# Gated edge pass: the weighting of the gathered rows and the absolute value of the angle move from VectorE to ScalarE

## The reference

```python
# layer 1, per edge (row = source, col = destination): a gate from both ends, then a gated sum
edge_weights = sigmoid(relu(concat([h[row], h[col]]) @ We1 + be1) @ We2 + be2)
aggr = segment_sum(edge_weights[:, None] * h[row], col, num_segments=n)
# layer 3, per edge: the time encoding, from the node's last update and the edge's time
rel_t = last_update[src] - t
rel_t_enc = cos(rel_t[:, None] * Wt[0][None, :] + bt)          # 64 columns
edge_attr = concat([rel_t_enc, msg])                           # 64 + 64 columns
```

## Time and profile before

| | us |
|---|---|
| median of three runs | 13884.4 (13879.9 to 13896.82) |
| the profiled execution | 13875.03 |
| its span | 13873.3 |
| DVE busy | 10723.6 (77%) |
| PE busy | 8685.8 (63%) |
| POOL busy | 6951.8 (50%) |
| ACT busy | 2809.5 (20%) |
| the gated pass, about 6616 to 8025 | 1409 |

### The profile page before, as it was taken

How to read it: one execution, slowest core, us unless ns; L and a number is a source line. 1 busy time by engine, 2 the same in 40 slices (tenths; PEclk the granted TensorE clock), 3 DMA queues, 4 the chain that set the end, 5 groups by cost and what they waited for, 6 DMA issues and landing times. The chain is left out here.

```text
span 13873.3 us, 209115 instructions
## 1 busy us (share of the span) xinstructions
PE 8685.8 (63%) x52858; PEld 7028.6 (51%) x52859; DVE 10723.6 (77%) x16335; ACT 2809.5 (20%) x4518; POOL 6951.8 (50%) x7719
## 2 busy tenths in 40 slices
PE   4663577767778678773566636773666665666664
PEld 3552255553566446553555524552555554555554
DVE  7666479964899559985888867998677877677777
ACT  0110222223222232220444412221000000000000
POOL 3774057730777227760777706773344443344442
PEclk8555788878788788886888856665788888788887
DMA  4335754437444464451555612222233333333333
GB/s 179 113 112 131 266 165 105 104 53 295 112 105 104 113 260 106 105 93 28 141 147 145 141 23 51 54 54 23 86 96 92 93 95 69 95 93 93 95 93 65
DMA packets 720170, 1523.50 MB, mean 110 GB/s; under 512 B 364796, under 2 KB 416585, under 8 KB 680627
## 3 DMA queue, kind: packets, MB, share of 16 engines
q0 software_dynamic: 306624, 795.04, 24.1%
q1 hardware_dynamic: 413427, 727.07, 15.4%
HBM read 1050.48 MB, written 471.10 MB: 110 GB/s over the span
## 5 line engine op out<-in xcount | busy, mean ns | idle before, releaser
L967 POOL DMA_INDIRECT h<-table,edges_ring x3984 | 3785.5, 950 | 1291.0 <-issue 1161.1
L1146 PE MATMUL bank<-h,edges_onehot 128*128 128x260 f32 (+1 forms) x7968 | 2150.6, 431 | 717.6 <-DVE acc L1307 396.4
L1146 PEld LDWEIGHTS bank<-h,edges_onehot 128*128 128x128 f32 x7968 | 1693.8, 263 | 1130.2 <-DVE acc L1307 458.7
L1241 DVE TENSOR_TENSOR_SCAN bank<-edges_fresh,edges_top,bank 4x1024 f32<-4x1024 bf16 x660 | 1542.0, 2336 | 426.8 <-PE bank L1121 426.8
L967 POOL DMA_INDIRECT edges_rows<-table,edges_ring x1512 | 1492.3, 987 | 465.0 <-issue 415.7
L1121 PE MATMUL bank<-ident,edges_score 128*4 128x128 f32 x5280 | 1017.2, 358 | 953.1 <-DVE edges_score L1271 797.3
L1248 DVE TENSOR_TENSOR_SCAN edges_top<-edges_fresh,bank 4x1024 f32<-4x1024 bf16 x660 | 1497.0, 2268 | 0.2
L956 POOL COPY edges_ring<-src_idx 128x8 uint32 (+1 forms) x440 | 90.7, 207 | 2759.4 <-PE bank L1146 1356.4
L1121 PEld LDWEIGHTS bank<-ident,edges_score 128*4 128x4 f32 x5280 | 495.9, 104 | 1266.9 <-DVE edges_score L1271 841.9
L1307 DVE TENSOR_TENSOR acc<-acc,bank 128x260 f32 (+1 forms) x2640 | 919.8, 348 | 206.1 <-DVE acc L1297 59.8
L2010 POOL DMA_INDIRECT rec<-dst,slots x782 | 797.1, 1019 | 433.6 <-issue 433.2
(11 more groups left out here) (345 smaller groups left out, 16680.7 us busy)
## 6 DMA issues: line engine op xcount, KB each, us to landing
table<-x SPq DMA_DIRECT2D x154, 1040.0 KB, 7.9
edge_score<-edge_feat SPq DMA_DIRECT2D x220, 512.0 KB, 3.7
table<-h SPq DMA_DIRECT2D x77, 1040.0 KB, 7.9
table<-source_typed_rows SPq DMA_DIRECT2D x63, 1040.0 KB, 8.1
h<-table,edges_ring POOLq DMA_INDIRECT x3984
edge_feat<-edge_score SPq DMA_DIRECT2D x110, 512.0 KB, 3.0
dst_row<-dst_rows SPq DMA_DIRECT2D x71, 704.0 KB, 4.2
buf<-rec SPq DMA_DIRECT2D x44, 840.0 KB, 5.2
```

Of the source, the lines that this page charges most:

```text
L967: pool.indirect_dma_start(out=rows[s % R][:, j, :], out_offset=None, in_=table, in_offset=bass.IndirectOffsetOnAxis(ap=ring[:, s * ST + j: ...
L1146: ins = pe.matmul(sum_b[k % 3], onehot[s][:, j, :], rows[s][:, j, A0:W], start=j == k * GT, stop=j == (k + 1) * GT - 1)
L1241: v.tensor_tensor_scan(score_b[0:HEADS, :], fresh[s][:, 0:SLOTS_SB], score_b[0:HEADS, :], top[1 - s][:, SLOTS_SB - 1:SLOTS_SB], ALU.add, A ...
```

## The change

ACT takes over two steps. The absolute value of the angle becomes an ACT instruction of its own in front of the Sin, with a semaphore between the two, `angle_folded`. The weighting of the rows becomes eight ACT instructions, one for each tile, each a Copy whose scale is the gate's column of that tile; they stand behind the Sigmoid, with a wait for it. DVE loses both instructions, and with them its wait for the gate. The count of chained DVE instructions per superblock goes from 9 to 8, since one link is now the last of the angle.

```diff
@@ scalar, step(n, o)
                     act.wait_ge(angle_made, u + 1)
                     hold(act, feat_flipped, u - 1)
 
+                    act.activation(angle[:, :, :], angle[:, :, :], ACT.Abs).then_inc(angle_folded, 1)
+                    act.wait_ge(angle_folded, u + 1)
                     act.activation(feat[s][:, :, 0:64], angle[:, :, :], ACT.Sin, bias=half_pi[:, 0:1], scale=-1.0
                                    ).then_inc(cos_made, 1)
...
                     act.wait_ge(dot_made, u + 1)
                     hold(act, rows_weighted, u)
                     act.activation(gate[:, :], dot[:, :], ACT.Sigmoid, bias=be2[:, 0:1]).then_inc(gate_made, 1)
+                    act.wait_ge(gate_made, u + 1)
+                    for j in range(ST):
+                        row = rows[n[1]][:, j, 0:D]
+                        ins = act.activation(row, row, ACT.Copy, scale=gate[:, j:j + 1])
+                    ins.then_inc(rows_weighted, 1)
@@ vector
-                L = 9
+                L = 8
...
-                        v.wait_ge(gate_made, u + 1)
-                        rh = rows[s][:, :, 0:D]
-                        v.tensor_tensor(rh, rh, gate[:, :].unsqueeze(2).to_broadcast([P, ST, D]), ALU.mult
-                                        ).then_inc(rows_weighted, 1)
-
...
-                        c.link(v.scalar_tensor_tensor(angle[:, :, :], turns[:, :, :], -C2, angle[:, :, :], ALU.mult,
-                                                      ALU.add))
-                        v.scalar_tensor_tensor(angle[:, :, :], angle[:, :, :], -1.0, angle[:, :, :], ALU.mult,
-                                               ALU.max).then_inc(angle_made, 1)
+                        v.scalar_tensor_tensor(angle[:, :, :], turns[:, :, :], -C2, angle[:, :, :], ALU.mult,
+                                               ALU.add).then_inc(angle_made, 1)
```

More of the change, by code:

```diff
@@ L1391, in gated_edges @@
         (ring_kept, onehot_made, onehot_flipped, flipped_kept, dst_spread, dot_made, gate_made, rows_weighted,
-         sums_made, sums_taken, chain, loaded, angle_made, cos_made, feat_flipped, featT_kept) = (
+         sums_made, sums_taken, chain, loaded, angle_made, angle_folded, cos_made, feat_flipped, featT_kept) = (
              p.semaphore(n) for n in (
                  "ring_kept", "onehot_made", "onehot_flipped", "flipped_kept", "dst_spread", "dot_made", "gate_made",
-                 "rows_weighted", "sums_made", "sums_taken", "chain", "weights_in", "angle_made", "cos_made",
+                 "rows_weighted", "sums_made", "sums_taken", "chain", "weights_in", "angle_made", "angle_folded",
+                 "cos_made",
                  "feat_flipped", "featT_kept"))
```

## The result

The changed kernel takes 13982.5 us (median of 4 runs, 13980.4 to 13988.1) against 13886.1 us (4 runs): ratio 1.0069, 95% interval 1.0052 to 1.0087. It is slower by 96 us; 13975 was forecast. The two profiled spans differ by 13981.4 - 13873.3 = 108 us.

What follows compares the result with a forecast made beforehand. DVE was busiest (88%), but the chain from angle through Sin to Sigmoid and weighting had little room. Lengthened, its loop summed to 13.16 to 14.2 us, taken as 13.5 against 12.66: 92 us more, 13975 forecast, range 13860 to 14110.

Steps and rivals of the forecast that it cites:

- The forecast's main step: On ACT, the Sin's table load would stand behind the Abs in all 110 superblocks, exposed for 1.29 us each.
- The loop: Sigmoid's end, eight Copies, first sums, take 0, angle, Abs, load, Sin, transposes, L1507, load, Sigmoid: 13.16 to 14.2 us.
- what DVE was spared: L1538 and L1579, 1.91 us per superblock off DVE, would become idle time at take 0 and take 3, worth nothing.
- a step of 13.5 us: Gated pass, per superblock: 13.5 us against 12.66, 0.84 us more, so 92 us over 110 superblocks.
- From the Copies to take 0: PE's first sum group up to take 0: 0.9 us at PE's lower clock, 0.75 at the higher.
- The transposes: Eight on PE after the Sin: 1.10 us, or 1.92 us in a third of superblocks, after about 2.4 us idle.
- The Abs: New ACT instruction of 512 columns ahead of the Sin: 0.61 us, bounds 0.58 and 0.72.
- the eight Copies: Weighting on ACT behind the Sigmoid: 2.56 us, bounds 1.9 and 3.2; 0.40 us for one Copy.
- What was said to cost nothing: L1498 queued behind the Copies: L1583 up to 0.7 us late, yet the dot at 11.5, before the Sigmoid asks at 12.9.
- The load ahead of the Abs: Rival on ACT: Sin's load goes before the Abs, early in three of four superblocks; about 13820 us, faster; chance 0.13.
- everything cheap: Rival: Copies 1.9 to 2.3 us, sums 0.75, transposes 1.10; step 12.4 to 12.9, no measurable change, 13884; chance 0.12.
- everything dear: Rival: PE at its lower clock around both idle times, Copies not overlapping; step 14.2 to 14.8, around 14080 us; chance 0.21.

Runs made afterwards that it cites:

- e3: The changed kernel plus a one-column Sin ahead of the wait for the angle, drawing the Sin's table load forward: ratio to before 0.9983 and 0.9994.
- e1: The changed kernel with the weighting back on DVE, so only the Abs is on ACT: ratio to the kernel before 0.9999 and 1.0003.
- e2: The changed kernel with the absolute value back on DVE, so only the eight weighting Copies are on ACT: ratio to the kernel before 0.9994 and 1.0005.
- e5: The changed kernel with ACT reporting every two weighted tiles and PE's sum group waiting only for its own two: ratio to the kernel before 1.0016.
- the first experiment: Each half of the change alone against the kernel before, e1 (0.9999; 1.0003) and e2 (0.9994; 1.0005).
- the changed kernel's second run: The changed kernel unaltered, timed again in the third later batch beside the kernel before: ratio 1.0045.

## Why the prediction was right

**The mechanism.** The forecast's main step was that the Abs, which waits for the angle, would leave the Sin's load behind it in all superblocks. The profile after shows it (load 0.7 us behind the Abs, 110 of 110), and e3 shows that without this load there is no loss: with it drawn forward the ratio falls from 1.0045 to 0.9983 and 0.9994. e1 and e2 show that neither the load nor the Copies cost anything alone there. The prediction has both in one loop; that either alone would cost nothing, it doesn't say. The loop was the one named, in the order named, and what DVE was spared turned into idle time, as said. For the first comparison itself the cause rests on the parts of the loop, which add up to the step; e3 was not timed there.

**The size.** 92 us were forecast for the pass by a step of 13.5 us; 13.64 were measured, 107 us. Two terms were off and in part made up for each other. The first was misread: the prediction calls 0.90 us its value at PE's lower clock, and 0.75 the one at the higher. The windows view of that stretch in the kernel before, from the end of L1538 to take 0, shows the higher clock:

```profile
8019.95:8020.87 0.92, 0.87 (x7) 0.87 (x8) 0.00 (x1) 0.00 (x0) 0.00 (x0) 1.00 0.00 0
```

- From the Copies to take 0: 0.90 forecast from the last superblock, 1.33 measured. At the higher clock the term is 0.92 to 0.98 us, at the lower 1.49, and no run shows 0.75. The lower one held in 74 of 109 superblocks. The 16 matmuls of the spread took 3.38 us in the superblock shown against 2.55, and the pass's clock is 0.79 against 0.82. PE's lower clock fell on the sums and the spread, right behind the long idle time at the Copies: the mean granted clock of the spread is 0.56 against 0.84 before. In the first sum group it is 0.66 against 0.61, so it was low in the kernel before as well, and the last superblock was the exception.
- The transposes: a third at 1.92 us was forecast. In the superblock shown they took 1.09 us, and over the pass 119 us of busy time for 880 against 131 before; only 1 set of eight in 110 took over 1.5 us, against 15 before. The idle time ahead of them was 1.15 us in the superblock shown and 1.56 us in the mean, not 2.4 us, because the spread ran later and longer. So the clock's cost came in another place than forecast.

The sum was 0.13 us too low: 0.43 us too little at take 0, 0.18 too much at the transposes, 0.13 too much at the Copies. That 13975 lies within 8 us of the measured time is luck in part. By the step 107 us were to be added and not 92; the medians differ by 96 because the profiled execution of the kernel before lay 11 us below its median.

**Prices.** The Abs took 0.63 us (0.61), the eight Copies 2.45 us (2.56, bounds 1.9 and 3.2), one Copy 0.387 us (0.40). A Copy starts (2.44 - 0.39) / 7 = 0.29 us behind the one before, an overlap of 0.09 us; the earlier trace rows show 0.06, and the prediction reckoned with 0.08.

**What was said to cost nothing.** L1584 waited for the spread up to 1.3 us (up to 0.7 forecast); the Sigmoid still didn't wait for the dot, so it did cost nothing. e3 shows how thin this cover was: with the loop shortened, the dot is the last to come in 61 of 110 superblocks.

**The rivals.** The load ahead of the Abs did not come about. Of "everything cheap" only the transposes' price came true (1.08 us in the mean); the Copies took 2.44 us and not 1.9 to 2.3. Of "everything dear" only the lower clock behind the Copies did, in two superblocks of three. The trace of the changed kernel, too, disagrees with the drain that the Trainium skill adds to a load ("ScalarE: Activation LUTs", section "What ACT_TABLE_LOAD costs"): the load at 7333.91 is followed by the Sin at 7335.21, 1.30 us later. The Trainium skill's rule that abs is in every set (same page, section "Table sets: the hidden batching unit") agrees with all runs: no Abs drew a load.

**What stays open.** How much each half costs alone, and what the early load gives, where PE's signals are prompt; by the forecast's arithmetic the theory of e1 gave 13.2 us a step for the Abs alone, but no run tested it there. And why PE's signals come late in the later batches.

## What to carry to other kernels

In all traces here the table load stands directly ahead of the function that needs it. Whether it is hidden depends on where the wait lies: in the function's own instruction, the load runs ahead of the wait; in a cheap function or a register instruction in front, it stands behind. So a cheap function put in front, with the wait on it, turns a hidden load into one that is waited for. In e5 a change of the count that ACT waits for was enough, so look again where the loads stand after every change. Relieving the busiest engine gains nothing if the work goes into the loop of waits that closes just behind it: add up the loop before and after, for every engine that it passes, and also the next loop, since that one takes over. If a load must lie in front of a wait, one instruction of one column of the same function ahead of the wait moves it there for 0.2 us.

## Unexpected on the hardware

The same program took 13886 us in one comparison and 16032 to 16654 us in the four later batches, on three chips. The chip of the first comparison isn't on record; one of the three had 16654 us in one batch and 16032 us in another, so it isn't a matter of the chip alone. The instructions of ACT and DVE lasted as long there (the Copies 387 ns, the loads 1283 ns, L1591 1220 ns). PE was busy longer, 9520 us against 8742 us for the changed kernel, and the granted clock over the whole program was 0.71 to 0.72 against 0.78. In the gated pass PE's semaphore signals arrived late, some as late as PE's next piece of work (the counts stand with the first experiment), and DVE's waits show it as "remote". In the changed kernel's second run:

```profile
DVE acc L1584 <- remote: 122.3, 42, 9.5
...
DVE edges_rows L1584 <- remote: 72.6, 22, 3.7
```

The ends of matmuls are modelled in such a trace, so it may be that the matmuls themselves ended late; no run here tells the two apart. Nor is the whole program explained by the gated pass: the changed kernel took 2164 us more in its second profiled execution, and a step longer by 0.99 us makes only 108 us of that. The other passes have waits on "remote" as well, but were not looked into. A difference of a few tenths of a per cent should be compared with both kernels in one batch, and one that is measured in this condition can come out smaller: the change cost 0.69% in the one condition and 0.45% in the other, though the intervals overlap (1.0052 to 1.0087 and 1.0028 to 1.0063).
